# Two layers of a post-norm decoder on one core: scales of the first quantised product by pairs of batches, energies of the context attention between its steps

## The reference, cut to what matters

```python
x = _layernorm(x + _L0_attn_ref(...))                       # causal attention
x = _layernorm(x + _L0_xattn_ref(x, fside, ctx_1024))       # the quantised block
x = _layernorm(x + _L0_ffn_ref(...))                        # ternary feed-forward
x = _layernorm(x + _L1_attn_ref(...))                       # window attention
x = _layernorm(x + _L1_xattn_ref(x, ctx_1024, ...))         # context attention
x = _layernorm(x + _L1_ffn_ref(...))                        # experts

def _smooth_quant_linear(x, w):                 # per batch: x [256, 256], w [256, 256]
    amax_x = max(abs(x), axis=0); amax_w = max(abs(w), axis=0)      # per channel
    s = maximum(sqrt(maximum(amax_x, EPS) / maximum(amax_w, EPS)), EPS)
    xs = x / s; ws = w * s
    x_scale = maximum(max(abs(xs), axis=-1), EPS) / 127             # per row
    w_scale = maximum(max(abs(ws), axis=-1), EPS) / 127
    x_q = clip(round(xs / x_scale)); w_q = clip(round(ws / w_scale))
    return x_q @ w_q.T * x_scale * w_scale.T

def _expert_forward(xe, guw, dw):               # _L0_xattn_ref: one expert per batch
    gate, up = split(_smooth_quant_linear(xe, guw))
    return _smooth_quant_linear(silu(gate) * up, dw)

def _L1_xattn_ref(x, features, Wq, bq, Wk, bk):
    energy = (features @ Wq.T + bq) @ (features @ Wk.T + bk).T      # does not depend on x
    return x @ softmax(energy)
```

## Time and profile before

| | |
|---|---|
| median of three runs | 507.15 us (505.82 to 510.51) |
| profiled execution | 511.0 us |
| its span, first to last instruction | 509.3 us |
| PE busy | 407.1 us, 80% |
| DVE busy | 345.2 us, 68% |
| ACT busy | 243.0 us, 48% |
| POOL busy | 107.5 us, 21% |
| mean granted clock of PE | 0.907 of 2.4 GHz |

### The profile page before, as it was taken

One profiled execution on the slowest core, in us unless ns is written; L12 is line 12 of the kernel. 1 busy time (PEld: TensorE's weight loads), 2 busy tenths in 40 slices (PEclk: granted clock), 3 DMA queues, 4 the chain that ended last, 5 costly groups with the idle time before them and its releaser, 6 DMA issues.

```text
span 509.3 us, 8075 instructions
## 1 busy us (share of the span) xinstructions
PE 407.1 (80%) x3090; PEld 316.1 (62%) x3090; DVE 345.2 (68%) x782; ACT 243.0 (48%) x433; POOL 107.5 (21%) x111
## 2 busy tenths in 40 slices
PE   1905477998884765589998688999988899999993
PEld 1605454676654644478767565667666678888883
DVE  0489687777776848686548888657846495666545
ACT  1558713655444674476567714445635324422220
POOL 4400004538511620051182000000001700000000
PEclk9967597999898586599999989999988999999997
DMA  6900020000000000000000006970000000000101
GB/s 201 295 6 1 1 69 5 2 3 3 2 0 2 0 2 0 0 1 0 3 0 1 1 1 87 117 147 3 2 1 0 0 2 1 0 1 0 43 1 42
DMA packets 13127, 13.33 MB, mean 26 GB/s; under 512 B 2905, under 2 KB 12449, under 8 KB 12833
## 3 DMA queue, kind: packets, MB, share of 16 engines
q1 hardware_dynamic: 12224, 12.54, 11.0%
q10 hardware_dynamic: 864, 0.27, 0.3%
HBM read 11.56 MB, written 1.05 MB: 25 GB/s over the span
## 4 chain that ended last, share of the span: by engine, by line
PE 59%; DVE 23%; ACT 11%; issue 3%; POOL 2%; DMA 1%; SPq 0%; DVEq 0%; POOLq 0%; ACTq 0%
PE PS L2148 11%; PE PS L2165 6%; ACT arena L751 5%; PE PS L1764 4%; PE PS L1848 4%; DVE mx L1266 4%; PE PS L1742 3%; PE PS L384 3%; PE PS L1889 3%; PE PS L1816 3%; PE PS L1645 2%; PE PS L1858 2%; PE PS L2089 2%; PE PS L2076 2%; DVE mx L1261 2%
## 5 line engine op out<-in xcount | busy, mean ns | idle before, releaser
L870 ACT ACTIVATE PT<-PS 128x512 f32<-128x512 f32 x96 | 53.5, 594 | 37.2 <-PE PS L1816 37.0
L2148 PE MATMUL PS<-arena_r 128*128 128x512 f32 x264 | 64.5, 393 | 1.5 <-ACT xT L751 1.5
L667 POOL TENSOR_SCALAR va<-mv 128x4 f32<-128x4 f32 x12 | 5.3, 442 | 272.5 <-DVE mv L1102 272.5
L1742 PE MATMUL PS<-ident,arena 128*96 128x128 bf16 x416 | 32.0, 245 | 29.6 <-DVE arena L1145 27.5
L2148 PEld LDWEIGHTS PS<-arena_r 128*128 128x128 f32 x264 | 48.1, 188 | 11.3 <-issue 2.2
L751 ACT ACTIVATE arena<-PS 96x1024 bf16<-96x1024 bf16 (+4 forms) x59 | 44.4, 810 | 20.7 <-PE PS L1742 13.2
L1742 PEld LDWEIGHTS PS<-ident,arena 128*96 128x96 bf16 x416 | 29.8, 144 | 33.7 <-DVE arena L1145 29.1
L1764 PE MATMUL PS<-masks,ident 128*128 128x512 bf16 x112 | 43.0, 384 | 5.1 <-DVE mx L1266 2.9
L1266 DVE TENSOR_REDUCE mx<-PS 128x4 f32<-128x1024 f32 x32 | 39.0, 1219 | 1.7 <-PE PS L1799 0.6
L2165 PEld LDWEIGHTS PS<-arena_r 128*128 128x128 f32 x264 | 34.4, 191 | 2.5 <-DVE arena_r L1567 0.9
L2165 PE MATMUL PS<-arena_r 128*128 128x256 f32 x264 | 35.1, 283 | 0.7 <-DVE arena_r L1567 0.7
(11 more groups left out here) (219 smaller groups left out, 911.9 us busy)
## 6 DMA issues: line engine op xcount, KB each, us to landing
arena<-in_L_ffn_w SPq DMA_DIRECT2D x16, 176.0 KB, 10.1
arena<-in_L_ffn_w SPq DMA_DIRECT2D x2, 1024.0 KB, 10.9
arena<-in_L_ffn_w SPq DMA_DIRECT2D x2, 704.0 KB, 6.7
arena<-in_fside_BxS2xS SPq DMA_DIRECT2D x1, 1024.0 KB, 12.5
out<-x SPq DMA_DIRECT2D x4, 256.0 KB, 2.5
x<-in_x SPq DMA_DIRECT2D x1, 768.0 KB, 8.8
arena<-in_L_attn_Wq SPq DMA_DIRECT2D x2, 256.0 KB, 4.3
arena<-in_L_attn_Wo SPq DMA_DIRECT2D x2, 256.0 KB, 5.9
```

The source lines that it names most:

```text
L870: nc.scalar.activation(PT[:, n % 2, 512 * j:512 * (j + 1)], bank(3 + j), ACT.Exp, scale=NEG_SCALE)\
L1742: last = nc.tensor.transpose(bank16(4 + n % 4, P, i * P, STK), s_, ident16[:, :])
L2148: last = mm(bank(2 * (n % 2) + gu), wp[c][:, gu, c_ * P:(c_ + 1) * P], xp[5][:, c, blk * 512:(blk + 1) * 512], start=(step == 0 and c == 0 ...
```

## The change

It makes the smoothing scales and the operands in two pairs of batches instead of all at once. The weights' maxima are two reductions; the ratios, roots and operands of batches 0 and 1 come before the application of the layer norm to batches 2 and 3, and those of batches 2 and 3 later, amid the steps of batches 0 and 1. `xqk` moves to another place in `arena` (words 11264 on, where `f_nat` was and `qT` comes later), and the energies move to banks 4 to 7. PE, DVE, ACT and POOL get new orders: energies, context maxima, exponentials and context scalings are put between the steps of the quantised product, the spreading of the row scales becomes a step of its own (`spread_row_scales`), and Silu of the first batches comes before the integers of the last. The arithmetic stays. The diff, with unchanged lines mostly left out:

```diff
-xqk = carve(0, [P, 2, B * S])
+xqk = carve(11264, [P, 2, B * S])
...
-    def smooth_roots(linear, n):
+    def smooth_roots(linear, lo, hi):
...
-        alone(pool.tensor_tensor(qs[:, 2, 0:n], qs[:, 0, 0:n], exponents[:, 1, 0:n], ALU.pow))
-        alone(pool.tensor_scalar(qs[:, 1, 0:n], qs[:, 2, 0:n], Q_EPS, None, ALU.max), root_ready)
+        alone(pool.tensor_tensor(qs[:, 2, lo:hi], qs[:, 0, lo:hi], exponents[:, 1, lo:hi], ALU.pow))
+        alone(pool.tensor_scalar(qs[:, 1, lo:hi], qs[:, 2, lo:hi], Q_EPS, None, ALU.max), root_ready)
...
+    smooth_roots(1, 0, 2 * DC)
     inverse_deviations(0, 2)
-    smooth_roots(1, B * DC)
-    pool.wait_ge(sums_inverted, 1)
-    for b in range(B):
+    smooth_roots(2, 2 * DC, B * DC)
+    def scaled_weights(b):
...
-    for b in range(B):
+    def gated(b):
...
-    smooth_roots(2, B)
+    pool.wait_ge(sums_inverted, 1)
+    scaled_weights(0)
+    gated(0)
+    scaled_weights(1)
+    gated(1)
+    scaled_weights(2)
+    gated(2)
+    gated(3)
+    scaled_weights(3)
+    smooth_roots(3, 0, B)
...
-    evac_xT(1, 2, 4)
-    for b in range(B):
+    def context_exponentials(b):
...
-            last = nc.scalar.activation(xP[:, b, k, :], bank(b, S, k * S), ACT.Exp,
+            last = nc.scalar.activation(xP[:, b, k, :], bank(4 + b, S, k * S), ACT.Exp,
...
+    context_exponentials(0)
+    evac_xT(1, 2, 4)
     integers(0)
+    context_exponentials(1)
     integers(1)
+    copy_row_scales(0)
     copy_qT(0)
+    copy_row_scales(1)
+    context_exponentials(2)
+    copy_qT(1)
+    context_exponentials(3)
     integers(2)
-    copy_qT(1)
+    silu(0)
     integers(3)
-    copy_row_scales(0)
-    copy_row_scales(1)
+    silu(1)
+    copy_row_scales(2)
     copy_qT(2)
+    copy_row_scales(3)
     copy_qT(3)
-    silu(0)
-    copy_row_scales(2)
-    silu(1)
-    copy_row_scales(3)
     silu(2)
     silu(3)
...
+    def weight_maxima(b):
+        v.tensor_reduce(amx[:, 1, b * DC:(b + 2) * DC], fT[:, b:b + 2, :, :].rearrange("p b c s -> p (b c) s"), X,
+                        ALU.max, apply_absolute_value=True)
+    def smooth_ratios(lo, hi):
+        link(v.tensor_scalar(amx[:, :, lo:hi], amx[:, :, lo:hi], Q_EPS, None, ALU.max))
+        link(v.reciprocal(qs[:, 0, lo:hi], amx[:, 1, lo:hi]))
+        v.tensor_tensor(qs[:, 0, lo:hi], amx[:, 0, lo:hi], qs[:, 0, lo:hi], ALU.mult).then_inc(ratio_ready, 1)
+    def smooth_scales(linear, lo, hi):
+        dve.wait_ge(root_ready, linear)
+        link(v.reciprocal(qs[:, 0, lo:hi], qs[:, 1, lo:hi]))
+    def scaled_operands(b):
+        for c in range(DC):
+            j = b * DC + c
+            v.tensor_scalar(xw[:, b, 0, c, :], xT[:, c, b * S:(b + 1) * S], qs[:, 0, j:j + 1], None, ALU.mult)
+            ins = v.tensor_scalar(xw[:, b, 1, c, :], fT[:, b, c, :], qs[:, 1, j:j + 1], None, ALU.mult)
+        ins.then_inc(Q["xw"], 1)
...
+        if L == 0:
+            copied_out(dve, NGM)
+            weight_maxima(0)
...
-            copied_out(dve, NGM)
-            v.tensor_reduce(amx[:, 1, :], fT[:, :, :, :].rearrange("p b c s -> p (b c) s"), X, ALU.max,
-                            apply_absolute_value=True)
+            weight_maxima(2)
...
-            channel_maxima(1)
+            link(channel_maxima(1))
+            smooth_ratios(0, 2 * DC)
...
-            norm_pair(0, 2)
+            norm_stats(0, 2)
+            smooth_scales(1, 0, 2 * DC)
+            scaled_operands(0)
+            scaled_operands(1)
+            norm_apply(0, 2)
...
-    for b in range(B):
+    def context_maxima(b):
...
-        v.tensor_reduce(xmx[:, b, :], bank(b).rearrange("p (t s) -> p t s", t=2), X, ALU.max,
+        v.tensor_reduce(xmx[:, b, :], bank(4 + b).rearrange("p (t s) -> p t s", t=2), X, ALU.max,
...
-    def smooth_scales(linear, n):
-        link(v.tensor_scalar(amx[:, :, 0:n], amx[:, :, 0:n], Q_EPS, None, ALU.max))
-        link(v.reciprocal(qs[:, 0, 0:n], amx[:, 1, 0:n]))
-        v.tensor_tensor(qs[:, 0, 0:n], amx[:, 0, 0:n], qs[:, 0, 0:n], ALU.mult).then_inc(ratio_ready, 1)
-        dve.wait_ge(root_ready, linear)
-        link(v.reciprocal(qs[:, 0, 0:n], qs[:, 1, 0:n]))
...
-    channel_maxima(2)
-    link(channel_maxima(3))
-    smooth_scales(1, B * DC)
-    for b in range(B):
-        for c in range(DC):
-            j = b * DC + c
-            v.tensor_scalar(xw[:, b, 0, c, :], xT[:, c, b * S:(b + 1) * S], qs[:, 0, j:j + 1], None, ALU.mult)
-            ins = v.tensor_scalar(xw[:, b, 1, c, :], fT[:, b, c, :], qs[:, 1, j:j + 1], None, ALU.mult)
-        ins.then_inc(Q["xw"], 1)
-    for b in range(B):
+    def row_scales1(b):
...
-        nat = PS[:, k:k + 2, :].rearrange("p a (t d) -> p (a t) d", t=2)
-        row_scales(b, nat, row_scales_ready)
-        if b == 0:
-            dve.wait_ge(Xs["exp"], B)
-            v.reciprocal(xsm[:, :, :], xsm[:, :, :]).then_inc(sums_inverted, 1)
-            v.tensor_reduce(amx[:, 1, 0:B], ctxT[:, :, :], X, ALU.max, apply_absolute_value=True)
-        else:
-            whole_numbers(b - 1)
-    whole_numbers(B - 1)
-    for b in range(B):
+        row_scales(b, PS[:, k:k + 2, :].rearrange("p a (t d) -> p (a t) d", t=2), row_scales_ready)
+    def scaled_product(b):
...
+    context_maxima(0)
+    row_scales1(0)
+    context_maxima(1)
+    row_scales1(1)
+    channel_maxima(2)
+    link(channel_maxima(3))
+    smooth_ratios(2 * DC, B * DC)
+    context_maxima(2)
+    whole_numbers(0)
+    context_maxima(3)
+    whole_numbers(1)
+    smooth_scales(2, 2 * DC, B * DC)
+    scaled_operands(2)
+    scaled_operands(3)
+    dve.wait_ge(Xs["exp"], B)
+    v.reciprocal(xsm[:, :, :], xsm[:, :, :]).then_inc(sums_inverted, 1)
+    v.tensor_reduce(amx[:, 1, 0:B], ctxT[:, :, :], X, ALU.max, apply_absolute_value=True)
+    row_scales1(2)
+    scaled_product(0)
+    row_scales1(3)
+    scaled_product(1)
+    whole_numbers(2)
+    whole_numbers(3)
+    scaled_product(2)
+    scaled_product(3)
...
-    smooth_scales(2, B)
+    smooth_ratios(0, B)
+    smooth_scales(3, 0, B)
...
-    for b in range(B):
+    def energies(b):
+        if b >= 2:
+            pe.wait_ge(xT_ready, turned(1, b))
...
-            last = mm(bank(b, S, k * S), xqk[:, 0, b * S + k * P:b * S + (k + 1) * P],
+            last = mm(bank(4 + b, S, k * S), xqk[:, 0, b * S + k * P:b * S + (k + 1) * P],
...
-    transpose_x(1, 2, 4)
     def scaled_to_rows(b):
...
-        if b < 2:
-            pe.wait_ge(Xs["exp"], 2 * b + 2)
-        if b >= 2:
-            pe.wait_ge(Q["q32"], b - 1)
+        if b == 2:
+            pe.wait_ge(Q["wbc"], 2)
+        elif b == 3:
+            pe.wait_ge(Q["q32"], 2)
...
-        elif b == 0:
-            pe.wait_ge(xT_ready, 8)
+        else:
+            pe.wait_ge(Xs["exp"], b + 3)
...
-        if b >= 2:
-            pe.wait_ge(Q["wbc"], b - 1)
-        else:
-            pe.wait_ge(Q["q32"], 3)
+    def spread_row_scales(b):
+        pe.wait_ge(Q["q32"], 3 if b >= 2 else 1)
+        pe.wait_ge(row_scales_ready, b + 1)
...
     scaled_to_rows(0)
+    energies(0)
+    energies(1)
     scaled_to_rows(1)
-    scaled_to_rows(2)
+    transpose_x(1, 2, 4)
+    energies(2)
+    energies(3)
+    spread_row_scales(0)
     quant_transposes(pe, 0)
-    scaled_to_rows(3)
+    spread_row_scales(1)
     quant_transposes(pe, 1)
     products(0)
+    scaled_to_rows(2)
     products(1)
+    scaled_to_rows(3)
+    spread_row_scales(2)
     quant_transposes(pe, 2)
+    spread_row_scales(3)
     quant_transposes(pe, 3)
     products(2)
     products(3)
```

## The result

| | before | changed |
|---|---|---|
| median | 506.88 us (4 runs) | 501.63 us (4 runs) |
| ratio, 95% interval | | 0.988, 0.983 to 0.993 |
| the profiled execution's time | 511.0 us | 502.09 us |
| its span | 509.3 us | 500.4 us |
| first context projection on PE starts | 149.06 | 145.92 |

A forecast was written before the change was run, and what follows sets the result against it. A relay of handovers between attention and feed-forward bounds the kernel: moving the second maxima from 188.65 to 185.3 gains 3.35 us, so the 507.15 us median becomes 503.8, range for 8 in 10 500.8 to 506.6.

The forecast's parts named there:

- the stage: Relay from the attention's end to DVE's second quantised product maxima: start moves from 188.65 to 185.3, a gain of 3.35 us.
- new wait for the last exponential: DVE, from 168.3 until ACT's last exponential at 170.0: 1.7 us, with row scales 2 and product 0 queued behind.
- table load in front of integers 3: ACT's Silu table load, 1.28 us, formerly behind all integers, would now lie ahead of integers 3.
- second load: ACT: if Silu's table lacked Identity, 1.28 twice more; gain 0.8, 506.4 us. With other losses, gain 0 to 2, chance 0.19.
- overlap of the tail: Stage's end: Silu, row copies and gating of the first batches beside the last integers, named as what gains; no separate size.
- head start of 10 us: First row scales on DVE start at 157.4 instead of 167.1; 1.7 us is left at integers 2 on ACT.
- Steps 2, 4 and 7: DVE delayed by POOL: layer norm power 1.1 us, second root 0.55, context scaling about 0.7; without the first two, gain 5.0.
- Step 7: Tail: whole numbers 3 on DVE meet POOL scaling context batch 1 and end at 179.95; about 0.7 us lost.
- PE's clock: Half clock from 164.8 to 173.7, full behind it; full throughout worth 0.5 at qT 0 and 0.3 at rows 3.
- half clock to the end: Bound on PE in the tail: half instead of full clock costs 0.55 us, making the gain 2.8.
- the second: POOL does not hold DVE up and PE stays at full clock: gain 5.1 to 6.3, about 501.5 us, chance 0.25.
- POOL's context scalings: Four ahead of gating 2; 1.07 us more each erases the gain, 2.27 total gives 508.8 us; slower, chance 0.03.

The follow-up runs named there:

- e6: Changed kernel with context maxima and row scales 2 ahead of DVE's wait for the last exponential, and rows before products on PE: stage 32.87 us, ratio to before 0.990.
- e7: Changed kernel with a Silu of one column in ACT's idle time, bringing the table load forward: stage 33.43 us, ratio to before 0.988.
- e5: Changed kernel with ACT's order put back, all four Silus behind integers, row scales and qT of batches 2 and 3: stage 38.54 us, ratio to before 1.000.
- e1: Changed kernel with two more powers of four columns on POOL ahead of the layer norm's, beside the eight operand scalings: stage 36.15 us.
- e2: Changed kernel with three additions of 256 columns on POOL ahead of the layer norm's powers, beside the operand scalings: stage 36.36 us.
- e8: Changed kernel with one extra power of 32 columns on POOL ahead of the layer norm's powers, beside the operand scalings: stage 39.27 us.
- e9: Changed kernel with six additions of four columns on POOL ahead of the layer norm's powers, beside the operand scalings: stage 35.55 us.
- e3: Changed kernel with new DVE and PE orders around the last exponential and the Silu table load brought forward: stage 32.11 us, ratio to before 0.981.
- before, once more: Kernel before the change, unedited and traced again: stage 39.60 us, projections starting at 150.47.

## Why the prediction was wrong

Right:

- That the stage is worth what it moves the second maxima, and that what lies behind shifts as it stands: 320.65 against 320.18 us from the mark to the end.
- The new wait for the last exponential: DVE waits 1.27 for it, 1.7 was written; e6 shows that this and the rows behind the product cost 1.43.
- The table load in front of integers 3, 1.28: it is there, and e7 gets 0.87 back. No second load came: integers 3 use Identity behind Silu and run at once, so that rival fell. The Trainium skill, ScalarE: Activation LUTs, "Table sets: the hidden batching unit", which has identity in every set, agrees.
- That most of the gain is the overlap of the tail (e5), and that the head start of 10 us is mostly eaten in the middle: integers 2 start 3.9 earlier than before, where 1.7 was written.

Wrong, in us of the sum:

1. **Steps 2, 4 and 7, the meetings of DVE with POOL, 1.1 + 0.55 + about 0.7 = 2.35: DVE lost nothing in them.** This is the step that failed, as the assumption that one engine waits for the other's whole instruction and that DVE pays. In steps 2 and 4 POOL's instruction is a power of four columns, while the rows shown for the meeting, had POOL at 256 or more. The prediction named as open whether four columns hold DVE for 1.04 us, put both ends of steps 2 and 4 into its bounds, and took the wrong one. e1, e2, e8 and e9 show that three additions of 256 columns cost three scalings 0.35 to 0.42 each, and a power of 5.62 us costs none. The one row on the power itself, 1.39 instead of 1.04, has POOL as the one that takes longer, and in the changed kernel it is so again: 1.18 for the power, and no DVE step longer than alone.

   Step 7 is another case, for there POOL does move 256 columns, and the number of columns does not explain that DVE got off. It had a fitting row: in the kernel before whole numbers already run beside the same context scalings, and the earlier trace rows have 0.847 at most against 0.679 alone, so 0.17 and not 0.7, while the earlier trace rows have POOL's scaling at 1.352 against 0.917. In the changed kernel whole numbers 3 take 0.69 and POOL 2.35 for two. Why POOL waits there and DVE in e2 no run shows. Step 7 had no second end in the bounds either: with steps 2 and 4 at nothing they give a gain of 5.0, and with step 7 as well it is 5.7.

   The Trainium skill, SBUF — State Buffer, "SBUF: two separate sides", calls the pair of ports that the two engines share a lock for the whole instruction. e2 agrees (a scaling that waits takes 0.70 to 0.77, with additions of 0.72 each); e1 and e8 do not, and here the measurement decides.
2. **PE's clock.** Transposes 0 ran at full clock (0.62, not 1.06), ACT worked without a gap from 154.77 on, and the last exponential ended at 164.70, which is 167.84 on the prediction's scale, not 170.0. That is 2.16 earlier, of which the prediction's own terms give 1.65 to the meetings of steps 2 and 4 and leave 0.5 for the clock. DVE's small steps behind it save another 0.1. In the tail it is the other way, half clock where full was taken: transposes 3 take 1.03 instead of 0.62 and product 3 takes 1.04 instead of 0.6, 0.85 together, where the bounds priced half clock to the end at 0.55. With some 0.2 of handovers that makes about 1.0.

Sum: 3.35 + 2.35 + 0.6 - 1.0 = 5.3, and 5.29 was measured. The 0.6 and 1.0 are read off the two schedules, not from a run that changes the clock alone, so the sum is an account and not a test. That the clock's two errors partly cancel is luck. Without the first error the sum would have been 5.7 and the forecast faster by over 1%. Of the rivals the second (no meetings, full clock; gain 5.1 to 6.3, 501.5, with 0.25) had the time and half the mechanism: the clock was not full. One slip changed no chance: POOL's context scalings would have used up the gain at 0.95 us more each, (3.35 + 0.45) / 4, and not at 1.07.

## What to carry to other kernels

When two engines are said to block each other, price the meeting by a row with the same two instructions and the same amount of data, read in it which of the two takes longer, and do not use a row where the other engine only takes as long; if there is none, that cost has two ends and the forecast hangs on it. Look for such a row in the kernel before first: here it was there for one of the three meetings. A head start made early in a relay is worth only what it lets the last steps do side by side: look at which engine does the steps behind the last batch. And compare stages between two marks when whole runs vary by more than the change: here the stage repeats within 0.02 us and the run by several.

## What the runs showed of the hardware

- A power of 32 columns on POOL takes 5.62 us beside eight DVE scalings that all run at 0.26 to 0.27 from start to start (e8); an addition of 256 columns, 0.72, stops one scaling for about 0.4 (e2).
- In other meetings POOL is the one that takes longer: two scalings of 256 columns took 2.35 instead of 1.84 beside one DVE step of 0.69 (changed kernel), and 2.73 and 2.84 in e7 and e3.
- A table load on ACT takes 1.28, and the first instruction that uses the table starts 0.01 behind it (169.54 and 170.83 in the changed kernel).
- The attention, whose code on PE no run changes, is followed by the projections at anything from 144.58 (e5) to 150.47 (before, once more). The granted clock of 84 to 110 us is 1.00 in the traces that start them by 147.5 (e6 the latest, 147.49), 0.87 to 0.88 where they start near 149, and 0.93 at 150.30 and 150.47.
